# A causal convolution's taps: four VectorE operations in place, or ScalarE products with GpSimd additions

## What is computed

```python
proj = layernorm(x) @ W_in + b_in                      # 512 -> 2 * 1024
hidden, gate = split(proj, 2)
conv = silu(sum(w[k] * padded[:, k:k + L, :] for k in range(4)) + b)   # causal, depthwise, 4 taps
dt_in, Bm, Cm = split(conv @ W_x, [128, 144])
delta = softplus(dt_in @ W_dt + b_dt)
# selective scan over time, 16 states n for each of the 1024 channels
h[t] = exp(delta[t] * A) * h[t-1] + delta[t] * conv[t] * Bm[t];  y[t] = sum_n h[t] * Cm[t]
x = x + layernorm((y + conv * d_param) * silu(gate) @ W_out + b_out)
x = x + layernorm(ffn(layernorm(x)))                   # two Hadamard-transformed, scaled projections, silu, one more
```

## Time and profile before

| what | us |
|---|---|
| median of 3 runs (lowest to highest) | 2864.34 (2860.25 to 2867.99) |
| the profiled execution: its time, and its span | 2862.8, 2861.0 |
| PE, DVE, ACT, POOL busy | 2522.2, 2279.4, 1821.8, 2085.8 |
| one steady chunk step (32 slots) | 155.8 |

### The profile page before, as it was taken

One profiled execution on the slowest core, in us unless ns is written; L12 is line 12 of the kernel. 1 busy time (PEld: TensorE's weight loads), 2 busy tenths in 40 slices (PEclk: granted clock), 3 DMA queues, 4 the chain that ended last, 5 costly groups with the idle time before them and its releaser, 6 DMA issues.

```text
span 2861.0 us, 45756 instructions
## 1 busy us (share of the span) xinstructions
PE 2522.2 (88%) x15760; PEld 2155.7 (75%) x15760; DVE 2279.4 (80%) x2584; ACT 1821.8 (64%) x3936; POOL 2085.8 (73%) x1714
## 2 busy tenths in 40 slices
PE   1546676999999999999999999999999999989987
PEld 0234555888888888888888888888888888877776
DVE  7817898888889888888888888988888989889321
ACT  0347776777767777767676776767676777755221
POOL 6228787878878797879787887878786978777221
PEclk8876998999999999999999999999999999999999
DMA  5651112565666666666656666666566565656586
GB/s 210 256 186 52 54 54 89 203 222 199 224 209 221 216 207 213 221 205 209 223 197 226 209 218 212 216 216 213 206 219 216 197 220 206 210 183 226 206 307 245
DMA packets 163879, 573.83 MB, mean 201 GB/s; under 512 B 17472, under 2 KB 19904, under 8 KB 129856
## 3 DMA queue, kind: packets, MB, share of 16 engines
q1 hardware_dynamic: 163648, 570.90, 58.0%
HBM read 536.75 MB, written 34.08 MB: 200 GB/s over the span
## 4 chain that ended last, share of the span: by engine, by line
PE 51%; DVE 22%; ACT 7%; POOL 5%; issue 5%; DMA 2%; DVEq 0%; POOLq 0%; ACTq 0%; SPq 0%
PE pF L652 15%; DVE h L999 11%; PE pM L597 10%; PE hT L584 9%; DVE acc L1010 7%; PE pD L665 7%; PE pM L634 7%; POOL dbx L1131 3%; DMA wug<-scratch_ug 2%; POOL conv L1187 2%; PE decay L652 1%; ACT L832 1%; PE hT L576 1%; ACT decay L832 1%; ACT delta L814 1%
## 5 line engine op out<-in xcount | busy, mean ns | idle before, releaser
L999 DVE TENSOR_TENSOR_SCAN h<-decay,dbx 128x512 f32<-128x512 f32 x1024 | 1203.2, 1207 | 294.0 <-ACT decay L832 237.0
L1131 POOL TENSOR_TENSOR dbx<-u,bb 128x2048 f32<-128x2048 f32 (+1 forms) x272 | 1177.8, 4331 | 81.0 <-DVE h L999 79.5
L832 ACT ACTIVATE decay<-delta,a_neg 128x255 f32<-128x255 f32 x2048 | 870.4, 467 | 207.4 <-DVE h L999 202.2
L652 PE MATMUL pF<-fxT_hi,wug 128*128 128x256 f32 x3840 | 749.4, 288 | 8.2 <-DMA wug<-scratch_ug 6.1
L584 PE MATMUL hT<-ident,h 128*128 128x128 f32 x4096 | 551.9, 279 | 130.3 <-DVE acc L1010 111.0
L584 PEld LDWEIGHTS hT<-ident,h 128*128 128x128 f32 x4096 | 481.0, 144 | 242.1 <-issue 160.2
L1010 DVE SCALAR_TENSOR_TENSOR acc<-hT,bcT,acc 128x1024 f32<-128x1024 f32 x480 | 606.6, 1264 | 34.8 <-PE hT L584 33.1
L652 PEld LDWEIGHTS pF<-fxT_hi,wug 128*128 128x128 f32 x3840 | 615.8, 192 | 11.5 <-DMA wug<-scratch_ug 8.9
L652 PE MATMUL pF<-fxT_lo,wug 128*128 128x256 f32 x1920 | 543.8, 283 | 0.0
L597 PE MATMUL pM<-xnT,w_in 128*128 128x256 f32 x2048 | 491.5, 384 | 10.9 <-ACT hid L773 3.4
L597 PEld LDWEIGHTS pM<-xnT,w_in 128*128 128x128 f32 x2048 | 375.5, 193 | 55.7 <-ACT hid L773 5.4
(11 more groups left out here) (113 smaller groups left out, 2511.3 us busy)
## 6 DMA issues: line engine op xcount, KB each, us to landing
wug<-scratch_ug SPq DMA_DIRECT2D x256, 1024.0 KB, 4.8
wd<-scratch_wd SPq DMA_DIRECT2D x256, 512.0 KB, 4.1
w_in<-in_W_in SPq DMA_DIRECT2D x256, 256.0 KB, 2.9
bb<-scratch_bc SPq DMA_DIRECT2D x128, 256.0 KB, 4.8
scratch_ug<-split_hi SPq DMA_DIRECT2D x8, 1024.0 KB, 5.9
scratch_ug<-split_lo SPq DMA_DIRECT2D x8, 1024.0 KB, 6.8
xb<-in_hidden_states SPq DMA_DIRECT2D x16, 512.0 KB, 4.9
xr<-in_hidden_states SPq DMA_DIRECT2D x16, 512.0 KB, 5.6
```

Source lines behind the costliest of these rows:

```text
L652: mm = pe.matmul(gate_up_bank(no)[:, which, :], wug[no % 2][:, 2 * which + a, kt, :], fxT[b][:, kt, :], start=(kt == 0 and i == 0), stop=( ...
L832: e = act.activation(da[q % 2][:, i, 1:], delta[c % 2][:, dt, 1:], ACT.Exp, scale=a_neg[:, dt, n:n + 1])
L999: dve.tensor_tensor_scan(row(h[n % 2][:, tiles, :]), row(da[q % 2][:, :, :]), row(dbx[n % 2][:, tiles, :]), 0.0, ALU.mult, ALU.add).then_i ...
L1131: pool.tensor_tensor(dbx[n % 2][:, tiles, :], u[:, tiles, :], rows, ALU.mult).then_inc(done if restarts(c) else prod_done, 1)
```

## The change

All four taps go to VectorE. For each channel tile it makes tap 3 with the bias by a tensor_scalar from hid into conv, then three scalar_tensor_tensor operations, each of which reads hid (shifted by k) and conv and writes conv in place; each waits for the one before. They stand in the same eight slots, behind `add_h` and `out_evac` and ahead of `silu_up`. ScalarE's `conv_taps`, GpSimd's `add_taps`, the tables `ACT_TAPS` and `POOL_ADDS` and the buffers tap go. GpSimd's `halo` (slot 18) now waits until the last tap is added.

```diff
-        ACT_TAPS = {8: 0, 9: 1, 10: 2, 12: 3, 13: 4, 14: 5, 15: 6, 16: 7}
+        DVE_TAPS = {8: 0, 9: 1, 10: 2, 12: 3, 13: 4, 14: 5, 15: 6, 16: 7}
-        POOL_ADDS = {5: (0,), 6: (1, 2), 7: (3, 4), 8: (5, 6), 9: (7,)}
...
@@ block.scalar
-            def conv_taps(j, dt):
-                act.activation(conv[j % 2][:, dt, :], hid[:, dt, HALO:], ACT.Identity, scale=taps[:, dt, HALO:HALO + 1],
-                               bias=b_conv[:, dt:dt + 1])
-                for k in range(HALO):
-                    e = act.activation(tap[dt % 2][:, k, :], hid[:, dt, k:k + T], ACT.Copy, scale=taps[:, dt, k:k + 1])
-                e.then_inc(tap_done, 1)
...
@@ block.vector
+            def conv_taps(j, dt):
+                if dt == 0:
+                    dve.wait_ge(halo_done, j + 1)
+                    if j >= 2:
+                        dve.wait_ge(y_gated, j - 1)
+                dve.wait_ge(m_evac, M_NO["hid", j, dt // 2] + 1)
+                dve.tensor_scalar(conv[j % 2][:, dt, :], hid[:, dt, HALO:], taps[:, dt, HALO:HALO + 1], b_conv[:, dt:dt + 1],
+                                  ALU.mult, ALU.add).then_inc(first_tap, 1)
+                dve.wait_ge(first_tap, DT * j + dt + 1)
+                for k in range(HALO):
+                    no = HALO * (DT * j + dt) + k
+                    if k:
+                        dve.wait_ge(tap_added, no)
+                    dve.scalar_tensor_tensor(conv[j % 2][:, dt, :], hid[:, dt, k:k + T], taps[:, dt, k:k + 1], conv[j % 2][:, dt, :],
+                                             ALU.mult, ALU.add).then_inc(tap_added, 1)
...
+                if front is not None and k in DVE_TAPS:
+                    conv_taps(front, DVE_TAPS[k])
                 if k == 1 and fold is not None:
                     silu_up(fold, HT - 1)
                 if k >= 3 and k % 2 and ff is not None:
                     silu_up(ff, (k - 3) // 2)
...
@@ block.gpsimd
             def halo(j):
+                wait_first(pool, tap_added, HALO * DT * j, pool_passed)
...
-            def add_taps(j, dt):
-                pool.wait_ge(tap_done, DT * j + dt + 1)
-                for k in range(HALO):
-                    no = HALO * (DT * j + dt) + k
-                    if k:
-                        pool.wait_ge(tap_added, no)
-                    pool.tensor_tensor(conv[j % 2][:, dt, :], conv[j % 2][:, dt, :], tap[dt % 2][:, k, :], ALU.add).then_inc(tap_added, 1)
```

More of the change, by code:

```diff
@@ L259, in fused_block @@
         hid = sb("hid", [P, DT, HALO + T])
-        tap = [sb(f"tap{i}", [P, HALO, T]) for i in range(2)]
         conv = [sb(f"conv{i}", [P, DT, T]) for i in range(2)]
@@ L301, in fused_block @@
         m_filled = sem("m_filled"); m_evac = sem("m_evac")
-        tap_done = sem("tap_done"); tap_added = sem("tap_added"); conv_done = sem("conv_done"); gate_done = sem("gate_done")
+        first_tap = sem("first_tap"); tap_added = sem("tap_added"); conv_done = sem("conv_done"); gate_done = sem("gate_done")
         bc_stored = sem("bc_stored")
@@ L894, in slot @@
                     normalise("z", fo, fo, fold, zn_done)
-                if front is not None:
-                    if k in ACT_TAPS:
-                        conv_taps(front, ACT_TAPS[k])
                 if cur is not None and k in ACT_GATE:
@@ L932, in front0 @@
                     hidden(0, pair)
-                    for dt in (2 * pair, 2 * pair + 1):
-                        conv_taps(0, dt)
                 conv_silu(0)
@@ L1076, in front0 @@
                 dve.tensor_scalar(a_neg[:, :, :], a_neg[:, :, :], -1.0, None, ALU.mult).then_inc(setup_d, 1)
+                for dt in range(DT):
+                    conv_taps(0, dt)
                 x_stats(1)
@@ L1224, in slot @@
                     moments("z", fold)
-                if front is not None:
-                    for dt in POOL_ADDS.get(n, ()):
-                        add_taps(front, dt)
                 if n == 9:
@@ L1254, in front0 @@
                 moments("x", 0)
-                for dt in range(DT):
-                    add_taps(0, dt)
                 halo(1)
```

## The result

The changed kernel takes 3160.72 us, the median of four runs (3158.09 to 3166.54), against 2864.32 for the kernel before. The ratio is 1.1038, with a 95% interval of 1.1016 to 1.106: slower by 296 us, where 291 were forecast. The profiled execution took 3158.9 us.

The account below looks back on a forecast made before the run. TensorE was taken as full in slots 8 to 17, VectorE becoming the bound. A steady step adds 14.8 + 11.1 - 5.3 - 1.3 = 19.3 us; with the other steps and front0, +292.4 on 2862.8 gives 3155 us, range 3077 to 3281.

Parts of the forecast that it names:

- The bound: Slots 8 to 17: TensorE without idle time, VectorE 5.3 us idle, the most that relieving ScalarE and GpSimd can give.
- The work: VectorE's four new operations for each channel tile: 1.85 us a tile, 14.8 us a step, bounds 11.7 and 18.5.
- The waits: Slots 9, 13 and 15: taps with two SBUF inputs wait for GpSimd's dbx, 3 x 3.7 = 11.1 us a step.
- the rival of eight collisions: Taps in even slots collide too: five more waits of 3.7 us in 15 steps, +277, 3432 us; chance 0.07.
- Slot 18: prod_hi no longer waits for TensorE and goes about 1.3 us earlier; the silu and VectorE's wait move up as much.
- `front0`: GpSimd is idle there; silu starts at 192.7 instead of 195.54, a gain of 2.8 us.
- The step 1 term: Step 1, with 3.0 us of VectorE idle time and no late TensorE, grows by 22.9 us.
- the step 2 term: Step 2, with 5.95 us of VectorE idle time in slots 8 to 17, grows by 18.65 us.
- TensorE's pauses: Slots 8 to 17: TensorE waits in its transposes, for acc_done and for silu_up, but is not late at slot 18.
- GpSimd's halo: Slot 18: halo waits about 7 us for the last tap; dbx of state 10 starts at most 1 us late.
- No collision: The Hadamard stage's wait doesn't touch these operations: a step costs 8.2 us, total +126, 2989 us; chance 0.11.
- VectorE never idles: All VectorE's idle time came from taps crowding ScalarE and GpSimd: steady step 149.4 us, total about 2775 us; chance 0.02.

Follow-up runs that it names:

- Experiment 5: Kernel before without taps 0 to 2 at all, ScalarE's products and GpSimd's additions both left out: 2859.3 us, 0.997.
- experiment 4: Changed kernel with constants 0.5 and 0.25 for the tensor_scalar's two per-partition scalars: 3153.25 us, 1.0993.
- experiment 1: Changed kernel, GpSimd starting dbx of states 6, 8 and 9 only after the colliding tile's first scalar_tensor_tensor: 3028.48 us, 1.0561.
- Experiment 2: Changed kernel with taps only in even slots, two tiles each in 8, 10, 12 and one each in 14, 16: 3008.92 us, 1.0492.
- experiment 7: Changed kernel with GpSimd's dbx of states 6, 8 and 9 cut into two instructions of 1024 columns: 3149.62 us, 1.0995.
- experiment 6: Changed kernel with the taps behind silu_up in odd slots: 3156.8 us, 1.1021.

## Why the prediction was right

**The bound.** TensorE and VectorE were both nearly full in slots 8 to 17, and the relief of the two others was counted as at most VectorE's 5.3 us of idle time. The new work used up 5.2 (the mean over steps 3 to 11): of VectorE's waits in these slots 0.1 us is left, and its other 1.4 us without work are gaps between instructions, most of them between the four of a tile, which are counted as work below. Experiment 5 shows that the relief by itself frees 0.4.

**The work.** Forecast 1.85 us a tile, 14.8 a step. A tensor_scalar that isn't held starts 1.89 us ahead of VectorE's next instruction, 15.1 a step. The sum hides a mis-sized term: the tensor_scalar takes 0.41 us, not 0.29. The rows at 32 and 128 columns gave the slope, and it holds for constants (0.29, experiment 4), but not for two per-partition scalars. The scalar_tensor_tensor takes 0.485 against 0.474. The overlap with the instruction behind a tile, 0.09 us where 0.02 were counted, and three gaps of 0.04 instead of four took most of the difference back, so that the sum came closer than its terms. The estimate by the formula in the Trainium skill (VectorE: DVE Perf Modes, on the errata), 0.424, was 0.06 too low for it, which is what a per-partition scalar adds in the earlier trace rows (474 against 411).

**The waits.** Forecast 3 x 3.7 = 11.1. In slots 9, 13 and 15 the tensor_scalar lasts 3.93, 3.91 and 3.80, and 0.65 in slot 8; over 0.41 that is 10.6, of which 0.2 are slot 8's, where no wait was forecast. The condition, that dbx starts as the odd slot's second scan ends and is running when the taps' turn comes, held in all 45 cases: it starts 0.1 to 0.65 us behind the scan, and 0.4 to 1.15 ahead of the tensor_scalar. In the even slots the margin was enough, and the rival of eight collisions got none of its five; experiment 1, which delays dbx, shows how it would begin.

**Slot 18** gave 1.3 us back, as forecast and for the reason forecast. The steady step: 15.1 + 10.6 - 5.2 - 1.3 = 19.2 us, forecast 19.3. Steps 0, 1 and 2 grew by 22.2, 20.0 and 20.1 (forecast 22.0, 22.9, 18.65), and `front0` gave 2.4 (2.8). Steps 3 to 14 grew by 233.4 together (231.6). The step 1 term was 2.9 too high and the step 2 term 1.5 too low, and part of this cancels.

**Two statements were off**, neither a term of the sum. TensorE's pauses wait for silu_up's product in the main (12.2 us in three waits in slots 8 to 17 of step 6), since the held taps stand ahead of it, and not for acc, which was named first. GpSimd's halo waits 4.8 to 5.0 us for the last tap from step 2 on, not 7 (7.2 and 7.4 in steps 0 and 1). Also, the chances of the forecast and its rivals add up to 1.01, so one of them is 0.01 too high.

**The rivals.** "No collision" was to give 2989 us. Experiment 2 is nearly that case, made by order alone, at 3009. Of the 20 us between, 4 are the kernel before, which was itself slower on that chip (2867.11 against 2862.8); the step takes 165.0 where 155.8 + 8.2 = 164.0 was forecast, and its short collisions (0.9) and the work (15.1 against 14.8) cover that. "VectorE never idles" fell with experiment 5.

## What to carry to other kernels

Before moving elementwise work to VectorE, look at what GpSimd runs at that moment: a float32 tensor_scalar on SBUF, or a scalar_tensor_tensor with two SBUF inputs, waits for the rest of the GpSimd instruction that is running (some 3.5 us of a dbx of 4.5, for an operation of 0.41). The queue order decides it: the same instructions in even slots take 152 us less. Not every operation on SBUF is held: the layer-norm statistics of x, which read one SBUF tile, start beside a long GpSimd instruction in 26 of 32 cases of the kernel before and take 0.67 us as ever. Relief of an engine counts only if something waits for it; leaving the work out altogether, as in experiment 5, is the cheapest way to learn the upper bound. A slot in which one engine is busy throughout may still be another's: before taking work out of it, look for an instance without that work.

## What was not expected of the hardware

- Per-partition scalars have a price in a short VectorE operation: 0.12 us for two at 256 columns (0.29 to 0.41), and it is hidden while the operation is held, which constants don't prevent (3.94 us, experiment 4).
- Two back-to-back GpSimd instructions and a VectorE queue take turns instruction by instruction (experiment 7), and short GpSimd ones are stretched too: prod_lo from 0.74 to 0.95.
- TensorE's granted clock fell to 0.87 in slots 8 to 17 of step 6, where it pauses for 12 of 68 us, and to 0.77 in step 0. Between two levels of 1.2 and 2.4 GHz that is some time at the lower one. VectorE was the bound there, and slot 18 and those behind it, at 1.00, show no cost. The place of the pause matters: in experiment 6 it comes later, TensorE works at 0.50 until shortly before slot 18, and that slot lasts 1.0 us longer.
